# Attention and FFN kernel: full-row products for the row maxima, two norms' Newton steps on GpSimd, exponential sums over all rows of each head

## The reference

```python
# x (2, 2048, 512); ctx (2, 128, 512); H = 16 heads of hd = 32
h = layernorm(x)                       # no gain
q, k, v = h @ Wq, ctx @ Wk, ctx @ Wv   # split into 16 heads
q, k = layernorm(q, gq, bq), layernorm(k, gk, bk)      # over the 32 of each head
attn = softmax(q k^T / sqrt(32))       # over the 128 keys
x = x + (attn v) @ Wo
s = layernorm(x) @ Win + bin_          # (.., 64)
h = relu(s[..., None] * W1 + b1)       # 16 inner values of each of the 64
g = sum(h * W2, -1) + b2
x = x + g @ Wout + bout
```

## Time and profile before

| | |
|---|---|
| median of 3 runs | 479.64 us |
| profiled execution | 481.05 us |
| its span, first to last instruction | 479.2 us |
| PE, DVE, ACT, POOL busy | 433.5, 358.1, 331.6, 204.4 us |
| mean granted clock of TensorE | 0.961 |
| chain that ended last | PE 69%, DVE 15%, issue 5%, ACT 5%, SPq 4% |

### The profile page before, as it was taken

How to read it: one execution, slowest core, us unless ns; L and a number is a source line. 1 busy time by engine, 2 the same in 40 slices (tenths; PEclk the granted TensorE clock), 3 DMA queues, 4 the chain that set the end, 5 groups by cost and what they waited for, 6 DMA issues and landing times.

```text
span 479.2 us, 7952 instructions
## 1 busy us (share of the span) xinstructions
PE 433.5 (90%) x2456; PEld 279.3 (58%) x2456; DVE 358.1 (75%) x742; ACT 331.6 (69%) x633; POOL 204.4 (43%) x189
## 2 busy tenths in 40 slices
PE   5699888999999999999999999999987998799924
PEld 2386656467376737675667647664653564357712
DVE  4799796687767996799678977695788637537885
ACT  3658747896828983798559856896479639653880
POOL 3326666345514551546253643276342502057300
PEclk9999989999999999999999999999996999799975
DMA  8552685771915187516941493119700690052004
GB/s 306 153 167 68 142 211 138 170 183 33 243 33 126 33 206 168 134 46 156 215 111 28 105 269 67 27 22 234 184 5 0 168 261 16 22 162 80 1 1 175
DMA packets 25290, 58.35 MB, mean 122 GB/s; under 512 B 5921, under 2 KB 6433, under 8 KB 22177
## 3 DMA queue, kind: packets, MB, share of 16 engines
q1 hardware_dynamic: 24992, 57.58, 45.7%
q10 hardware_dynamic: 256, 0.26, 0.2%
HBM read 22.18 MB, written 8.39 MB: 64 GB/s over the span
## 4 chain that ended last, share of the span: by engine, by line
PE 69%; DVE 15%; issue 5%; ACT 5%; SPq 4%; POOL 0%; DMA 0%; DVEq 0%; ACTq 0%; POOLq 0%
PE bank L1929 33%; PE bank L2028 8%; PE bank L1935 7%; PE bank L2016 6%; PE bank L1994 4%; DVE bank L841 4%; PE bank L2096 3%; DVE mx L769 2%; ACT hid L1433 2%; PE bank L2081 2%; PE bank L2031 2%; DVE ssq L757 2%; DVE ln L665 1%; PE bank L2040 1%; PE bank L2003 1%
## 5 line engine op out<-in xcount | busy, mean ns | idle before, releaser
L769 DVE TENSOR_REDUCE mx<-bank 128x4 f32<-128x512 f32 x128 | 83.1, 684 | 22.2 <-PE bank L1994 22.0
L1353 ACT ACTIVATE prob<-bank 128x512 f32<-128x512 f32 x128 | 72.3, 596 | 31.1 <-PE bank L2016 29.1
L520 POOL TENSOR_TENSOR qt_lo<-u,qt_hi 128x512 fp32r<-128x512 f32 x32 | 41.3, 1293 | 70.5 <-ACT u L1330 70.3
L1433 ACT ACTIVATE hid<-s_in,b_col,w_col 128x256 f32<-128x256 f32 x128 | 68.2, 597 | 1.9 <-DVE s_in L821 1.5
L2028 PE MATMUL bank<-prob,v_kv 128*32 128x512 f32 x256 | 66.8, 620 | 0.1
L2031 PE MATMUL bank<-prob,den_sel 128*32 128x512 f32 x256 | 66.3, 621 | 0.0
L841 DVE SCALAR_TENSOR_TENSOR bank<-hid,w_col,bank 128x256 f32<-128x256 f32 x120 | 58.1, 485 | 6.9
L1929 PE MATMUL bank<-wq_hi,zt_hi 128*128 128x512 f32 x128 | 55.3, 432 | 3.0 <-DVE wq_lo L683 3.0
L2016 PE MATMUL bank<-q_stack,k_stack 97*128 97x512 f32 x128 | 50.8, 446 | 7.0 <-DVE att L796 5.9
L513 POOL TENSOR_TENSOR u<-u,lnq 128x512 f32<-128x512 f32 x32 | 32.9, 1050 | 53.8 <-DVE lnq L670 53.8
L525 POOL TENSOR_TENSOR at_lo<-att,at_hi 128x512 fp32r<-128x512 f32 x28 | 35.4, 1281 | 39.3 <-ACT at_hi L1405 39.3
(11 more groups left out here) (158 smaller groups left out, 899.0 us busy)
## 6 DMA issues: line engine op xcount, KB each, us to landing
q_stack<-qt_hi SPq DMA_DIRECT2D x64, 256.0 KB, 4.9
xin<-in_x_dram SPq DMA_DIRECT2D x36, 256.0 KB, 3.9
q_stack<-qt_lo SPq DMA_DIRECT2D x32, 256.0 KB, 4.7
x<-in_x_dram SPq DMA_DIRECT2D x28, 256.0 KB, 4.7
out_dram<-x SPq DMA_DIRECT2D x28, 256.0 KB, 3.3
att<-in_L_xattn_Wk_dram SPq DMA_DIRECT2D x1, 1024.0 KB, 6.5
x<-in_L_xattn_Wq_dram SPq DMA_DIRECT2D x4, 256.0 KB, 7.4
hid<-in_L_xattn_Wv_dram SPq DMA_DIRECT2D x1, 1024.0 KB, 10.2
```

The source lines that it names most:

```text
L520: pool.tensor_tensor(qt_lo[:, :, cols], u[:, j, :].rearrange("p (i n) -> p i n", i=HC), qt_hi[:, :, cols].bitcast(F32), ALU.subtract).then ...
L769: dve.tensor_reduce(mx[:, j, :].rearrange("p (g i) -> p i g", g=G)[:, 2 * half:2 * half + 2, 2 * r:2 * r + 2], maxs_banks[T][half][j][r][: ...
L1353: act.activation(prob[:, h % PR, :], score_bank[t][h][:, :], ACT.Exp, scale=SCALE).then_inc(exp_done, 1)
L1433: act.activation(hid[:, hh % RR, :], of_half(s_in), ACT.Relu, bias=b1_col[:, hh:hh + 1], scale=w1_col[:, hh:hh + 1]).then_inc(hid_done, 1)
```

## The change

It does five things.

- `max_scores` takes all 128 partitions: `k_diag` is 512 columns wide, one quarter for each head row, and a call makes two matmuls of 128 partitions and 512 columns. `row_max` is the same size and count, with another access pattern.
- `newton1` and `newton_q` go from VectorE to GpSimd, as 7 and 5 small operations; `newton2` stays on VectorE. `square` has one buffer instead of two and waits for the `sum_squares` of the tile before.
- `values(t, c)` makes the products of the four heads of a chunk in the four column groups of one bank; `denominators(t, c)` multiplies the same four heads with 32 columns of ones into a second bank, so that each sum already stands on all 32 rows of its head. `spread`, `rden_high`, `rden_split`, `move_att` and the selectors go. Logarithm, exponential, error, fix and `normalise` are made for each chunk (four times a block), and `normalise` reads the product from PSUM.
- The ring `prob` has 8 heads; to make room, `lnq`, `win_in`, `wout_in`, `ctx_t` and `inv_d` lie in other buffers, and `scratch` goes. `exponential(t, h)` waits for the whole chunk that held its place.
- All orders and bank tables are new. In the prologue `project_q(0, 0, 0)` waits for two of the four `wq_low`, and `fold_bias`, which waits for the last of the parameter loads, stands at the end of VectorE's prologue and not ahead of `wq_low(3)`. `residual2` of a block comes after the whole rden work of the next.

```diff
-PR = 4
+PR = 8
-        k_diag = sb("k_diag", [P, HC, 2 * KV], F32R)
+        k_diag = sb("k_diag", [P, HC, G * KV], F32R)
-        squares = sb("squares", [P, 2, D])
+        squares = sb("squares", [P, D])
+        lnq = s_in[:, HT * P:].rearrange("p (a n) -> p a n", a=4)
...
+            def newton(buf, v, n_in, act_sem, act_value, step_sem, base):
+
+                w, y, a, c2 = (buf[:, n, :] for n in range(4))
+                pool.wait_ge(act_sem, act_value)
+                pool.tensor_scalar(w, v, EPS * n_in, None, ALU.add).then_inc(step_sem, 1)
+                pool.tensor_tensor(a, y, y, ALU.mult).then_inc(step_sem, 1)
+                pool.wait_ge(step_sem, base + 2)
+                pool.tensor_tensor(a, a, w, ALU.mult).then_inc(step_sem, 1)
+                pool.wait_ge(step_sem, base + 3)
+                pool.tensor_scalar(a, a, -0.5 / n_in, 1.5, ALU.mult, ALU.add).then_inc(step_sem, 1)
+                pool.wait_ge(step_sem, base + 4)
+                pool.tensor_tensor(c2, y, a, ALU.mult).then_inc(step_sem, 1)
+
+            def newton1(T):
+                newton(ln1, mv1[:, :, 1], 1, ln1_act, T * 2 + 2, ln1_step, T * 7)
+                pool.tensor_scalar(shift1[:, :], mv1[:, :, 0], -1.0, None, ALU.mult).then_inc(ln1_step, 1)
+                pool.wait_ge(ln1_step, T * 7 + 6)
+                pool.tensor_tensor(shift1[:, :], shift1[:, :], ln1[:, 3, :], ALU.mult).then_inc(ln1_step, 1)
...
-                for i in range(2):
-                    for r in range(2):
-                        rows = slice(2 * HD * r, 2 * HD * (r + 1))
-                        ins = pe.matmul(maxs_banks[T][half][j][r][:, 2 * KV * i:2 * KV * (i + 1)],
-                                        qt_hi[rows, 2 * half + i, j * P:(j + 1) * P], k_diag[rows, 2 * half + i, :],
-                                        start=True, stop=True)
+                for r in range(2):
+                    ins = pe.matmul(maxs_banks[T][half][j][r][:, :], qt_hi[:, 2 * half + r, j * P:(j + 1) * P],
+                                    k_diag[:, 2 * half + r, :], start=True, stop=True)
...
+            def values(t, c):
+
+                pe.wait_ge(exp_done, t * H + HC * (c + 1))
...
+                for i in range(HC):
+                    n = HC * c + i
+                    ins = pe.matmul(at_bank[t][c][HD * i:HD * (i + 1), :], v_kv[kv_of(t)][:, n * HD:(n + 1) * HD],
+                                    prob[:, n % PR, :], start=True, stop=True)
                 ins.then_inc(pv_done, 1)
+            def denominators(t, c):
+
+                for i in range(HC):
+                    ins = pe.matmul(den_bank[t][c][HD * i:HD * (i + 1), :], ones[:, :], prob[:, (HC * c + i) % PR, :],
+                                    start=True, stop=True)
+                ins.then_inc(pv_done, 1)
...
+            def rden_error(t, c):
+
+                dve.wait_ge(rden_act, t * C + c + 1)
+                dve.scalar_tensor_tensor(out=den_bank[t][c][:, :], in0=den_bank[t][c][:, :], scalar=-1.0,
+                                         in1=rden[:, c % 2, :], op0=ALU.mult, op1=ALU.mult).then_inc(rden_step, 1)
+
+            def rden_fix(t, c):
+
+                dve.wait_ge(rden_step, t * C + c + 1)
+                dve.scalar_tensor_tensor(out=rden[:, c % 2, :], in0=den_bank[t][c][:, :], scalar=2.0,
+                                         in1=rden[:, c % 2, :], op0=ALU.add, op1=ALU.mult).then_inc(rden_done, 1)
...
+                dve.tensor_tensor(att_of(T)[:, c, :], at_bank[T][c][:, :], rden[:, c % 2, :], ALU.mult).then_inc(att_done, 1)
...
             def iteration(t):
+                pe.wait_ge(exp_done, t * 16 - 8)
+                values(t - 1, 1)
...
+                denominators(t - 1, 1)
...
+                max_scores(t, 1, 1)
+                if t >= 2:
+                    pe.wait_ge(rden_done, t * 4 - 3)
+                scores(t - 1, 8)
+                scores(t - 1, 9)
...
+                max_scores(t, 1, 2)
...
+                scores(t - 1, 10)
+                pe.wait_ge(att_done, t * 4 - 3)
+                scores(t - 1, 11)
+                scores(t - 1, 12)
...
+                max_scores(t, 0, 2)
```

More of the change, by code:

```diff
@@ L538, in prologue @@
                 centre_wq(1)
+                newton1(0)
                 centre_wq(2)
@@ L589, in iteration @@
                     att_low(t - 2, 3)
-                square(t + 1, 3)
+                newton1(t + 2)
+                newton_q(t + 1)
             def epilogue():
@@ L2379, in iteration @@
+                values(t - 1, 3)
+                pe.wait_ge(exp_done, t * 16 + 2)
+                denominators(t - 1, 3)
+                project_q(t + 2, 2, 1)
+                pe.wait_ge(zt_lo_done, t * 4 + 12)
+                scores(t, 2)
                 pe.wait_ge(u_done, t * 4 + 10)
                 turn_q(t + 1, 3)
-                project_q(t + 2, 2, 1)
-                pe.wait_ge(mx_done[0], t * 8 + 12)
-                spread(t - 1, 2)
-                pe.wait_ge(att_done, t * 4 - 2)
@@ new lines, in epilogue @@
+                values(5, 1)
+                pe.wait_ge(exp_done, 89)
+                denominators(5, 1)
+                pe.wait_ge(mx_done[1], 51)
+                max_scores(6, 0, 2)
+                pe.wait_ge(exp_done, 90)
+                scores(5, 10)
+                pe.wait_ge(mx_done[1], 52)
+                project_o(4, 0, 0)
+                pe.wait_ge(exp_done, 91)
+                scores(5, 11)
+                project_o(4, 0, 1)
+                pe.wait_ge(att_done, 21)
+                project_o(4, 1, 0)
@@ new lines, in epilogue @@
+                pe.wait_ge(mx_done[0], 53)
+                pe.wait_ge(rden_done, 21)
+                max_scores(6, 1, 2)
+                project_o(4, 1, 1)
+                pe.wait_ge(mx_done[0], 54)
+                project_o(4, 2, 0)
+                pe.wait_ge(mx_done[1], 53)
+                pe.wait_ge(rden_done, 22)
+                max_scores(6, 0, 3)
+                pe.wait_ge(att_done, 22)
+                scores(5, 12)
+                project_o(4, 2, 1)
+                pe.wait_ge(x1_done, 17)
@@ new lines, in epilogue @@
+                turn_q(7, 0)
+                pe.wait_ge(att_done, 23)
+                pe.wait_ge(exp_done, 96)
+                max_scores(7, 0, 0)
+                pe.wait_ge(z2t_done, 20)
+                scores(6, 0)
+                pe.wait_ge(mx_done[0], 57)
+                scores(6, 1)
+                pe.wait_ge(rden_done, 23)
+                turn_q(7, 1)
+                pe.wait_ge(mxt_done, 7)
+                scores(6, 2)
+                pe.wait_ge(exp_done, 98)
+                max_scores(7, 0, 1)
@@ new lines, in epilogue @@
+                pe.wait_ge(g_done, 5)
+                project_y(4, 0)
+                pe.wait_ge(exp_done, 101)
+                project_y(4, 1)
+                pe.wait_ge(exp_done, 102)
+                scores(6, 6)
+                pe.wait_ge(rden_done, 24)
+                pe.wait_ge(qf_done, 31)
+                max_scores(7, 0, 2)
+                pe.wait_ge(out_done, 18)
+                scores(6, 7)
+                values(6, 0)
+                pe.wait_ge(exp_done, 103)
+                denominators(6, 0)
@@ new lines, in epilogue @@
+                pe.wait_ge(out_done, 19)
+                pe.wait_ge(att_done, 24)
+                max_scores(7, 1, 1)
+                pe.wait_ge(mx_done[0], 62)
+                scores(6, 8)
+                turn_q(7, 3)
+                pe.wait_ge(exp_done, 104)
+                values(6, 1)
+                pe.wait_ge(mx_done[1], 59)
+                denominators(6, 1)
+                pe.wait_ge(exp_done, 105)
+                pe.wait_ge(out_done, 20)
+                max_scores(7, 1, 2)
@@ new lines, in epilogue @@
+                project_y(5, 1)
+                pe.wait_ge(exp_done, 121)
+                scores(7, 10)
+                pe.wait_ge(out_done, 21)
+                scores(7, 11)
+                pe.wait_ge(exp_done, 122)
+                values(7, 1)
+                pe.wait_ge(out_done, 23)
+                denominators(7, 1)
+                pe.wait_ge(exp_done, 124)
+                scores(7, 12)
+                scores(7, 13)
+                pe.wait_ge(rden_done, 29)
+                scores(7, 14)
```

1709 lines of the change are left out of this document (775 added, 934 removed).

## The result

The changed kernel takes 483.26 us in the median (479.9 to 486.06) against 479.64, a ratio of 1.008 with a 95% interval of 1.006 to 1.010: slower by 0.8%, where 463.6 was forecast. Its profiled execution took 482.69, span 480.9, so 1.7 us more span than before. The other two microseconds of the medians are not in this one profile. The 17 runs go roughly with the mean granted clock of TensorE: the quickest, 479.9 us, has 0.966, the slowest, 486.06, has 0.945, the profiled one 0.960.

A forecast was written before the change was run, and what follows sets the result against it. The prediction took TensorE to bound the iterations (90% busy overall) and VectorE to lead the filling phase. Start -6.0, iterations -6.0 and end -4.0 sum to -16.0 us, 479.64 to 463.6, with a range of 450 to 477.

The forecast's parts named there:

- TensorE's list: TensorE's work in an iteration: full rows +1.9, no spread -0.9, fewer changes of division -2.7; 49.4 to 47.6 us.
- old 0.85 us wait: TensorE's wait in an iteration for row maxima that stood behind newton1 on VectorE; it goes, -0.9 us.
- full-row call: One max_scores call on TensorE: two passes of 0.23, 0.46 us, for 0.23 of bare pairs; +1.9 us an iteration.
- Newton steps: newton1 and newton_q, stretched beside GpSimd, leave VectorE: -3.7 us busy an iteration; 11.3 us off its list up to 74 us.
- GpSimd's small steps: The 12 moved operations take 0.2 us each, 2.4 an iteration; GpSimd goes from 23.4 to 26 of 50, never the bound.
- New waits: Iteration's head: TensorE waits for rden_fix (0.6 us) and for two row_max and normalise (0.7); taken as +1.5 us an iteration.
- A: Rival: new waits take the iteration's whole gain and the end gains nothing, only the start counts; 473.6 us, chance 0.16.
- B: Rival, slower: each chunk holds two banks until normalise; 0.85 us exposed per chunk costs 27 us, 490.6; chance 0.11.
- Start: Filling phase: half of VectorE's relief, -4, and -2 from the first project_q starting 2.6 us earlier; -6.0 us, bounds 0 and -12.
- First iteration: Forecast 1.2 us shorter, like each full iteration; TensorE's list there 1.6 us shorter.
- End: From 327 us: TensorE's list 3.3 us shorter, waits for spread's banks gone; -4.0 us, bounds -9 and 0.
- rival C: Tiling rule decides: divided products are worth 0.23 us a call, changes of division not saved; about 477 us, chance 0.03.

The follow-up runs named there:

- e1: The changed kernel with GpSimd's order edited: all four norm_q ahead of add_bout, and the add_bout beside newton2 waiting until newton2 is through; 472.9 us, ratio 0.986.
- e7: The kernel before with only newton1 and newton_q moved to GpSimd, behind square(t + 1, 3); 481.7 us (478.6 before on that chip).
- e3: The changed kernel without the Newton correction of 1/sum (rden_error and rden_fix left out); 484.0 us, ratio 1.010.
- e10: e1 with the first project_q waiting for all four wq_low again, as in the kernel before; 472.7 us (e1: 472.9).
- e2: The changed kernel with max_scores in half rows again, four products of 64 partitions and 256 columns; 488.9 us, ratio 1.019.
- e11: e1 with max_scores in half rows, the edit of e2; 478.8 us, ratio 0.9995.
- e8: The kernel before with full-row products in max_scores alone, two of 128 partitions and 512 columns; 481.0 us, ratio 1.004.
- e5: e1 with the add_bout beside newton2 waiting for aggregate2 instead, so that they run beside newton2; 485.4 us.

## Why the prediction was wrong, point by point

**TensorE's list: right in the main.** The forecast was 49.4 to 47.6 us an iteration, -1.8 (its three terms add to -1.7). e1's iteration is 49.16 against 50.96, which is also -1.8, but by luck: the old 0.85 us wait is gone in it and 0.5 of a new one has come, so the list alone is 1.45 shorter. What was sized too low is the full-row call. Behind a projection its two matmuls start 0.23 apart and the next projection takes 0.23, as forecast; behind a score, a transpose or a group of values the first takes 0.31 to 0.34, which is most of the calls in the new order.

Of the 19.7 us between 463.6 and 483.3, 10.4 go with the next step (e1 takes 472.9). The 9.3 that are left are mainly the start (7.3 in e1's profile) and the first iteration (2.4).

**The step that failed: the Newton steps.** The forecast read the stretching in the earlier trace rows rightly, but charged it to `newton1` and `newton_q`, as if it would leave VectorE with them. It belongs to whichever small step runs beside a large GpSimd operation. Of 3.7 us an iteration that should have left VectorE, 1.8 came back on `newton2`, the larger part of why it is busy 43.7 in the new iteration where 41.3 was forecast. And on `newton2` it costs TensorE directly, since `spread_rstd` comes right behind: 1.2 us in iterations 2 to 4, 2.8 in the fifth, 2.4 for block 5. The forecast even said that `newton2`'s steps would be stretched, and gave it no price. It walked along GpSimd's order and named `add_bout` and `norm_q` as waiting behind `newton_q`, but not what they would collide with: the edit that did it, `add_bout` ahead of `norm_q`, has no term in the sum.

**GpSimd's small steps: a size.** 0.20 to 0.27 us on 4 columns, 0.24 to 0.38 on 64; 3.6 us an iteration from first to last instead of 2.4. GpSimd at 26.2 of 50.5 as forecast. What matters is their place in the queue, as e7 shows with 0.9 us an iteration.

**New waits: a third.** 1.5 us at the head were forecast, 0.5 are seen (for `rden`), and none for `normalise`. With e3, where the chain is 1.4 shorter and nothing changes, and e1, where the iteration gets its 1.8 with the chains as they are, rivals A and B are refuted as mechanisms. The slower result that B forecast came true by something else.

**Start: wrong, -6 forecast, +1.3 measured.** The first `project_q` is at 21.0, near the forecast (20.5). But the phase isn't led by VectorE to its end: e7 took the same steps off VectorE and gained nothing there. The last key transfer in SP's queue lands at 78.5 in both kernels. The changed kernel waits for it:

```profile
78.67 0.47 PE L1999 MATMUL bank<-q_stack,k_stack 97*128 97x512 f32 x1 [2.74 <-issue]
```

The kernel before came to `scores(0, 0)` at 79.1 without a wait, since its list has `project_q(2, 1, 1)` and `turn_q(1, 2)` ahead of it. In the new list these 1.7 us stand behind it. So 0.4 us is won up to `scores(0, 0)`, and 1.7 are added behind: the +1.3. What is won ahead of `scores(0, 0)` is lost there (e10). No run puts the two calls back ahead of it. The forecast never read SP's queue, which the order of GpSimd and VectorE feeds. `fold_bias` was costed at nothing since it was "far behind"; beside `wo_lo` it took 3.0 us and TensorE 2.2 of them.

**First iteration: +1.2 instead of -1.2.** TensorE's list is 1.6 shorter there by the same prices, so 2.8 us came from elsewhere. 1.4 of them are four waits of 0.3 to 0.4 us, three for the row maxima, where the kernel before has none; the rest isn't placed. Neither e3 nor e1 changes it (34.06 and 34.08). Which of the new orders is to blame stays open.

**End: -4 forecast, +0.1 measured, -3.1 in e1.** The list is 3.3 shorter as counted, and e1 shows it. What ate it in the changed kernel was again `newton2`, of block 5: TensorE waits 2.4 for it. It is also granted a mean clock of 0.82 from 357 to 425, where the earlier trace rows have 0.88, but e1 has 0.83 from 350 to 420 and still ends 3.1 shorter. The waits of the earlier trace rows did not go, as was forecast, but changed their names: between 328 and 430 the changed kernel waits 4.6 us for `rden` and `normalise` and 4.5 for `exponential`.

**The tiling rule (rival C).** By the Trainium skill, TensorEngine Tiling (Array Packing), Overview, the half-row form should be the faster one. e2, e11 and e8 put full rows at between 0.45 us an iteration faster and 0.06 slower, so the changes of division eat the double speed of 64-row products here. With the stretches at 1.2 GHz that came with the half-row form in e11, full rows are worth 1.3% between e1 and e11.

## What to carry to other kernels

A small VectorE operation that reads only SBUF costs 0.16 us alone and up to the whole length of the GpSimd operation beside it; so a reordering of GpSimd is a change to VectorE's chains. List the small chains on which TensorE waits (here `newton2` with `spread_rstd` behind it), and look for what GpSimd has at that moment; an order and a wait that keep GpSimd off them were worth 2.1%. Before a start is credited with a gain, find the first point where TensorE waits for a queue that the change doesn't shorten: here the 24 transfers ahead of `scores(0, 0)`.

## What the hardware showed that was not expected

The held steps can be told by their ends. Of VectorE's operations on 64 columns or fewer that stay in SBUF (4 columns take 0.16 us alone), those that last over 0.3 us, 21 in the kernel before and 23 in the changed one, all end just behind a GpSimd operation: 0.02 to 0.04 us behind its end, and once 0.08.

A granted clock of 1.2 GHz came in the iterations behind nothing more than the small gaps of their head in e2 and e11, the two kernels whose `max_scores` divides the array in the new order (6.8 us in e11, 3 us lost), though not in the iterations of the kernel before, which changes division as often. Behind a wait of 2.8 us for `newton2` it came in e2, e3 and e5 and not in the changed kernel. No run here tells why.

Removing 39 us of VectorE's work from a kernel in which VectorE is 87% busy beside TensorE changed the iteration by 0.01 us (e3), while 1.8 us in the wrong place cost 1.3.
